# Issuing both halves of x from ScalarE's queue, and bias and gates from SyncE's

## The reference, cut to what matters

```
x = x + tanh(g_xattn[0]) * L0_xattn(layernorm(x), ctx, Wq, bq, Wk, bk)
# L0_xattn: query = ctx @ Wq.T + bq ; key = ctx @ Wk.T + bk      (both from ctx)
#           att   = softmax(query @ key.T) ; result = att applied to layernorm(x)
x = x + tanh(g_ffn[0])   * L0_ffn(layernorm(x), ...)    # ternary weights, 704 wide
x = x + tanh(g_xattn[1]) * L1_xattn(layernorm(x), ...)  # 16 heads
x = x + tanh(g_ffn[1])   * L1_ffn(layernorm(x), ...)    # 64 experts, top 8, and a shared one
```

## Time and profile before

| what | value |
|---|---|
| median of three runs | 623.46 us (622.93 to 625.71) |
| the profiled execution's own time | 623.48 us |
| its span, first to last instruction | 621.7 us |
| TensorE, VectorE, ScalarE, GpSimd busy | 97%, 76%, 68%, 37% |
| mean granted TensorE clock | 0.999 of full |
| all transfers | 56.47 MB, 91 GB/s over the span |

### The profile page before, as it was taken

One profiled execution on the slowest core, in us unless ns is written; L12 is line 12 of the kernel. 1 busy time (PEld: TensorE's weight loads), 2 busy tenths in 40 slices (PEclk: granted clock), 3 DMA queues, 4 the chain that ended last, 5 costly groups with the idle time before them and its releaser, 6 DMA issues.

```text
span 621.7 us, 11583 instructions
## 1 busy us (share of the span) xinstructions
PE 604.4 (97%) x3634; PEld 522.1 (84%) x3634; DVE 474.9 (76%) x1133; ACT 423.1 (68%) x1080; POOL 232.9 (37%) x280
## 2 busy tenths in 40 slices
PE   8789989999999999999999999999999999999997
PEld 6556879999999999999998888888887888887886
DVE  4999887777777688778775787778877777777775
ACT  5998979888888888789897435364544444443442
POOL 6699797766666566566653020000000000000000
PEclk9999999999999999999999999999999999999999
DMA  8332220100000000000030454453856466555630
GB/s 298 141 102 71 65 71 26 53 1 2 2 2 2 2 2 2 1 2 1 3 116 13 128 169 144 131 157 103 215 166 168 117 173 166 164 155 148 195 127 34
DMA packets 33653, 56.47 MB, mean 91 GB/s; under 512 B 12800, under 2 KB 13504, under 8 KB 33600
## 3 DMA queue, kind: packets, MB, share of 16 engines
q1 hardware_dynamic: 33312, 55.82, 29.9%
q10 hardware_dynamic: 288, 0.00, 0.0%
HBM read 53.45 MB, written 1.31 MB: 88 GB/s over the span
## 4 chain that ended last, share of the span: by engine, by line
PE 85%; DVE 6%; POOL 5%; issue 2%; ACT 1%; DMA 1%; DVEq 0%; SPq 0%; ACTq 0%
PE bank L289 25%; PE bank L291 24%; PE bank L290 24%; PE bank L867 4%; PE bank L842 2%; PE bank L834 2%; POOL w L528 1%; POOL u L516 1%; DMA wqk<-in_qk 1%; DVE attT_lo L1860 1%; DVE stats L1680 1%; PE bank L714 0%; DVE rowmax L1848 0%; DVE hs L1774 0%; POOL rk L534 0%
## 5 line engine op out<-in xcount | busy, mean ns | idle before, releaser
L1395 ACT ACTIVATE inter_hi<-inter 128x512 fp32r<-128x512 f32 x63 | 39.8, 632 | 140.5 <-DVE inter L1959 140.5
L289 PE MATMUL bank<-xnT_hi,front_hi 128*128 128x512 f32 (+1 forms) x260 | 102.0, 392 | 0.0
L291 PE MATMUL bank<-xnT_hi,front_lo 128*128 128x512 f32 (+1 forms) x260 | 101.7, 391 | 0.0
L290 PE MATMUL bank<-xnT_lo,front_hi 128*128 128x512 f32 (+1 forms) x260 | 101.7, 391 | 0.0
L1963 DVE TENSOR_TENSOR inter_lo<-inter,inter_hi 128x512 fp32r<-128x512 f32 x63 | 43.6, 692 | 37.5 <-ACT inter_hi L1395 37.0
L1352 ACT ACTIVATE att<-bank,shift,rq 128x256 f32<-128x256 f32 x128 | 71.3, 571 | 0.0
L1848 DVE TENSOR_REDUCE rowmax<-bank 128x2 f32<-128x512 f32 x64 | 43.7, 686 | 27.4 <-PE bank L291 27.3
L550 POOL TENSOR_TENSOR att<-att,rowinv 128x512 f32<-128x512 f32 x60 | 62.0, 1053 | 5.2 <-DVE rowinv L1865 5.2
L534 POOL TENSOR_TENSOR rk<-msq,minus_half 128x4 f32<-128x4 f32 x32 | 32.9, 1027 | 78.9 <-DVE msq L1837 78.9
L1932 DVE TENSOR_TENSOR prod<-gate_s,bank 128x512 f32<-128x512 f32 x63 | 43.3, 687 | 21.9 <-PE bank L291 19.8
L290 PEld LDWEIGHTS bank<-xnT_lo,front_hi 128*128 128x128 f32 x260 | 48.9, 188 | 11.3
(11 more groups left out here) (266 smaller groups left out, 1802.0 us busy)
## 6 DMA issues: line engine op xcount, KB each, us to landing
w_all<-w_rows SPq DMA_DIRECT2D x128, 128.0 KB, 2.9
raw<-in_expert_w SPq DMA_DIRECT2D x32, 384.0 KB, 3.6
wvo_raw<-in_expert_w SPq DMA_DIRECT2D x16, 384.0 KB, 3.5
e_more<-in_expert_w SPq DMA_DIRECT2D x16, 384.0 KB, 3.6
raw<-in_head_qk SPq DMA_DIRECT2D x8, 384.0 KB, 3.4
wvo_raw<-in_head_vo SPq DMA_DIRECT2D x4, 384.0 KB, 3.1
w_keep<-in_head_vo SPq DMA_DIRECT2D x4, 384.0 KB, 3.0
gate_raw<-in_gate_wT SPq DMA_DIRECT2D x2, 704.0 KB, 8.8
```

The source lines that it names most:

```text
L289: pe.matmul(out, l_hi, r_hi_, start=start, stop=False, skip_group_check=True)
L290: pe.matmul(out, l_hi, r_lo_, start=False, stop=False, skip_group_check=True)
L291: return pe.matmul(out, l_lo, r_hi_, start=False, stop=stop, skip_group_check=True)
L1395: act.activation(inter_hi[:, slot, :], inter[:, slot, :], ACT.Copy).then_inc(a_Ihi, 1)
```

## The change

The two transfers of x go from SyncE to ScalarE, where they are the first two; bias and gates go from ScalarE to SyncE, behind wqk0 and ahead of gate_raw. Semaphores, sizes and everything else stay.

```diff
@@ block.sync
             sp.dma_start(ctxT_raw[:, :], ctxT).then_inc(l_ctxT, 16)
             sp.dma_start(wqk0[:, :, :], qk0).then_inc(l_qk0, 16)
-            for h in range(2):
-                sp.dma_start(x[:, 4 * h:4 * h + 4, :], x_tok[:, 4 * h:4 * h + 4, :]).then_inc(l_x[h], 16)
+            sp.dma_start(bqk[:, :], bias0).then_inc(l_small, 16)
+            sp.dma_start(gains_raw[:, :], gains).then_inc(l_small, 16)
             for k in range(KH):
                 sp.dma_start(gate_raw[:, k, :], gate_wT[:, k, :]).then_inc(l_gate[k], 16)
@@ block.scalar
-            act.dma_start(bqk[:, :], bias0).then_inc(l_small, 16)
-            act.dma_start(gains_raw[:, :], gains).then_inc(l_small, 16)
+            for h in range(2):
+                act.dma_start(x[:, 4 * h:4 * h + 4, :], x_tok[:, 4 * h:4 * h + 4, :]).then_inc(l_x[h], 16)
             high_ctxT()
```

## The result

The changed kernel takes 627.75 us, the median of eight runs (626.85 to 629.01), the kernel before 624.27 beside it (622.86 to 627.18). The ratio is 1.0052, with a 95% interval of 1.0033 to 1.007: slower, by 3.2 us as that ratio has it (the two medians are 3.48 us apart), at the bound of what can be told. The forecast was 628.2 with a range of 624.3 to 629.8. Where a term of a few microseconds is read, the lowest runs are named beside the median.

A forecast was written before the change was run, and what follows sets the result against it. The prediction took the opening chain from wqk0's landing through query_key, energy and the row maximum as the bound. A later wqk0 (3.2 us) plus TensorE's lower clock (1.6) gave 4.8 on 623.48, taken as 628.2, range 624.3 to 629.8.

The forecast's parts named there:

- The chain and x: Opening: wqk0's landing moves the end one for one; x has 0.5 and 3.2 us in hand, its early arrival worth nothing.
- One sign: Expected in the profile after: both halves of x land before or with wqk0.
- Issuing, bias and gates: Queue starts: two transfers replace two on each issuer, and bias and gates follow wqk0; nothing, up to 0.5 us if cover failed.
- The cover: Query_key work between wqk0's landing and copy_qk, 1.55 us, hides the landing of bias and gates.
- The bytes ahead of wqk0: Two queues alternate row by row: 0.967 MB of x and 0.655 MB precede wqk0's end, 1.62 MB; 3.2 us later.
- 1622 KB are reached at 7.87: Opening transfers: at the earlier kernel's rate these bytes have moved by 7.87, so wqk0 lands at 8.35.
- the lower bound of 1.7: wqk0's delay if all transfers after 3.0 ran at 433 GB/s: landing at 6.8, later by 1.7 us.
- Whole shares in turn: Rival on queue sharing: engines take whole shares, 1.18 MB ahead, wqk0 at 7.26, later by 2.15, 625.6 us; chance 0.10.
- The clock: TensorE idle 3.6 us before query_key loses its faster clock; query_key and energy slower by 0 to 4.2 us, taken as 1.6.
- Not slower: Rival: the opening's slow rate belongs to each queue, x fills gaps, wqk0 lands by 5.1 to 6.1; 623.5 to 624.5; chance 0.17.
- the sum of 4.8: Whole kernel: 3.2 us for wqk0's later landing plus 1.6 for TensorE's clock.
- The median: Base of the forecast: the profiled execution's 623.48 us, said to be the median to 0.02 us.

The follow-up runs named there:

- half the bytes: Changed kernel with only x's first half on ScalarE, the second on SyncE behind bias and gates, and 13 warming calls: 625.62 us, ratio 1.0015 to the kernel before.
- quarter-size rows: Changed kernel with x in eight transfers of one tile each, rows of 1024 bytes in place of 4096: 627.71 us, ratio 1.0073.
- tiny rows in front: Changed kernel with bias and gates issued first on ScalarE, then both halves of x, SyncE issuing neither: 626.29 us, ratio 1.0032.

## Why the prediction was right, point by point

*The chain and x.* Right. x early is worth nothing, and the landing of wqk0 moves the end; the shift of 4.80 us at 13.14 is 4.35 at the end. One sign was wrong without harm: the second half of x landed at 8.4, not before or with wqk0.

*Issuing, bias and gates.* Right in that they cost nothing (1.0005, 0.999 to 1.002, for them alone). SyncE issues gate_raw at 2.91 in place of 2.59, which nobody feels. The cover is thinner than the 1.55 us that I named: with 16 warming calls and full clock it was the landing of the gates, at 8.8, that ended ScalarE's first wait, and energy still started 2.7 us after query_key.

*The bytes ahead of wqk0.* The mechanism and the bytes were right: 0.93 MB of x had moved beside it against 0.967 forecast, and the runs with half the bytes (6.6), with quarter-size rows (6.0) and with tiny rows in front (5.2) put the landing near where the turn row by row does. Mis-sized was the step "1622 KB are reached at 7.87": I read the rate from the kernel before, where 1.25 MB had moved by 7.0; with two queues it was 1.56 MB, a third of the lead gained from 6 to 7 alone (402 GB/s against 295). The landing was 2.44 us later, not 3.2, about halfway to the lower bound of 1.7.

*Whole shares in turn.* Fell, though its landing at 7.26 was nearer to the measured 7.55 than my 8.35, and though 105 rows against 100, the landing with tiny rows in front (5.2) and the one with half the bytes (6.6) would fit it too. Two things do not. ctxT_raw, whose share comes first on each engine, would have landed about when it did before; it landed 1.70 us later, next to the first half of x. And 0.93 MB of x moved beside wqk0 where one share is 0.524, and 0.27 MB with rows of 1024 bytes where one share is 0.13. The rule of the Trainium skill ("DMA: Bandwidth & Descriptors", section "Queues, rings and completion order") that an engine drains a packet of typically 9 to 17 descriptors before it switches does not hold for these transfers; the measurement decides.

*The clock.* Right that query_key would run at the lower level, mis-sized in the sum: "I take 1.6" was 2.36 in the profiled execution and 2.3 to 2.5 in the two runs that isolate it (16 warming calls in the changed kernel, no warming in the kernel before). Wrong was the picture of a clock that falls in the idle time: the loads of the warming matmuls took 0.286 us and more to their end, as before, so the faster level had not come yet when TensorE fell idle at 4.92, and no record shows it between there and 13.1. query_key ran cold to its end, as it does with no warming at all. So the idle time of 1.74 us at 20.00, on a TensorE at full clock, was the wrong row to compare with, also in the rival "Not slower", where I let a gap of 1.3 us pass as free: with rows of 1024 bytes the gap was 1.2 us, and query_key took 4.39 us. Three of the eight runs, at 626.9 to 627.2 with a mean clock of 0.997, lie 0.7 lower and may have reached the faster level sooner; they have no trace. The two errors, 0.8 too much for the landing and 0.8 too little for the clock, cancelled in the sum of 4.8. That the sum meets the 4.80 of the trace is luck; that both terms are there is shown.

*The median.* I took the kernel before at 623.5, where its lower group lies; of the eight runs beside the change four lie at 622.9 to 623.5 and four at 625.1 to 627.2, so that the median came out between, at 624.27. So the ratio of medians, 3.2 to 3.5 us, is less than the 4.35 between the two traces, whose kernel before was an execution of the lower group.

## What to carry to other kernels

Before a transfer goes to a queue of its own "in parallel", ask which transfer is wanted first and how large the rows beside it will be: what is wanted first should have the engines alone, and on one queue the written order gives it that. A delay at the start can cost twice, once as itself and once as TensorE staying or going cold while it waits; warming matmuls that last until the data lands take the second part away. With 16 calls six of seven runs lay within 0.22 us of each other, though with 13, and wqk0 sooner, the runs still fell into two groups. And read the slack of a transfer at its first reader's next wait, not at its own: x's landing ended an idle time of 7.89 us and had 0.5 us in hand.

## What the runs showed of the hardware that was not expected

- In these transfers two queues share the DMA engines row by row, so eight bytes count as much as 4096: the small rows ahead of x kept 1 MB away from wqk0 (5.2 against 7.55), and without them wqk0 came 0.4 us sooner than in the kernel before, for 0.003 MB.
- A queue does not come in when its transfer is issued: behind gate_raw's issue, x waited at least 3.6 us for its first row.
- Two queues together moved 402 GB/s where one had 295 in the same microsecond. Why is not shown. It is not that every tensor comes slowly at first: gate_raw, which follows x in the kernel before, moved at 413 GB/s in its first microsecond, from 8 to 9 us.
- The clock column of a profile can show 1.00 where the weight loads take 0.34 us, as from 9 to 10 us in the changed kernel; their duration is the surer sign.
